# One block for the gated update and the three convolutions of a graph network

## The reference, cut to what matters

```
n   = relu(layernorm(x))
# layer 2: gated update
msg = segment_sum over edges of (n[src] @ W_msg.T + b_msg + edge_embed[edge_type])
r, z = sigmoid(...msg, n...);  new = tanh(i_n + r * h_n)      # GRU cell
x   = x + (1 - z) * new + z * n
n   = relu(layernorm(x))
# layer 3: three graph convolutions with symmetric norm (dinv = 1 / sqrt(degree))
y   = conv(conv(conv(n)))        # relu after the first two
x   = x + y
```

## Time and profile before

| | us |
|---|---|
| median of 3 runs | 6237.64 (6236.5 to 6240.86) |
| the profiled execution | 6241.27 |
| its span, first to last instruction | 6239.5 |
| PE busy | 4667.4 (75%) |
| POOL busy | 3137.0 (50%) |
| DVE busy | 2634.3 (42%) |
| ACT busy | 1472.9 (24%) |
| mean granted TensorE clock | 0.774 of full speed |

### The profile page before, as it was taken

How to read it: one execution, slowest core, us unless ns; L and a number is a source line. 1 busy time by engine, 2 the same in 40 slices (tenths; PEclk the granted TensorE clock), 3 DMA queues, 4 the chain that set the end, 5 groups by cost and what they waited for, 6 DMA issues and landing times. The chain is left out here.

```text
span 6239.5 us, 90775 instructions
## 1 busy us (share of the span) xinstructions
PE 4667.4 (75%) x25783; PEld 3126.0 (50%) x25784; DVE 2634.3 (42%) x6089; ACT 1472.9 (24%) x2786; POOL 3137.0 (50%) x3319
## 2 busy tenths in 40 slices
PE   5555555555555548888888888888899799999998
PEld 3444444444444435555555555555444444444444
DVE  6666666666666554444444444444312300000000
ACT  4211111111111123333333333333211211111000
POOL 3577777777777727777777777776000000000000
PEclk9555555555555568888888888888799899999999
DMA  6333333322333324444344434443345365555554
GB/s 218 110 94 94 94 94 94 92 87 84 93 94 94 105 80 125 132 133 133 125 131 133 133 123 133 133 133 96 136 159 162 99 200 191 187 193 190 192 193 150
DMA packets 337345, 817.56 MB, mean 131 GB/s; under 512 B 126590, under 2 KB 147633, under 8 KB 321059
## 3 DMA queue, kind: packets, MB, share of 16 engines
q1 hardware_dynamic: 217996, 516.64, 24.6%
q0 software_dynamic: 105568, 215.74, 12.7%
q10 hardware_dynamic: 13696, 84.07, 3.6%
HBM read 701.15 MB, written 114.23 MB: 131 GB/s over the span
## 5 line engine op out<-in xcount | busy, mean ns | idle before, releaser
L1388 POOL DMA_INDIRECT parts<-scratch_table,parts x1616 | 1541.2, 954 | 588.0 <-issue 480.1
L970 POOL DMA_INDIRECT parts<-scratch_table,parts x1616 | 1527.7, 945 | 554.5 <-issue 491.9
L185 PE MATMUL e_win<-parts 128*128 128x64 f32 x3232 | 783.0, 424 | 987.5 <-DMA parts<-scratch_table,parts 980.4
L185 PEld LDWEIGHTS e_win<-parts 128*128 128x128 f32 x3232 | 720.2, 328 | 1058.0 <-issue 1027.7
L1759 PE MATMUL c_sums<-ring,parts 128*128 128x512 bf16 (+1 forms) x3822 | 790.4, 368 | 21.0 <-ACT parts L2055 17.7
L1496 DVE TENSOR_TENSOR parts<-e_p,parts 128x512 f32<-128x512 f32 x404 | 279.4, 691 | 1160.5 <-PE e_p L1439 961.7
L185 PEld LDWEIGHTS e_win<-e_onehot,e_msg 128*128 128x128 f32 x3232 | 476.2, 211 | 245.3 <-issue 214.8
L1759 PEld LDWEIGHTS c_sums<-ring,parts 128*128 128x128 bf16 x3822 | 361.7, 98 | 430.1 <-issue 27.0
L1419 PE MATMUL e_p<-h,we 64*128 64x512 f32 x808 | 282.8, 772 | 365.7 <-DMA h<-in_edge_T 361.6
L222 DVE TENSOR_SCALAR parts<-e_iota,dst_rel,weight 128x64 f32<-128x64 f32 x1616 | 443.0, 335 | 254.8 <-issue 254.2
L1426 PE MATMUL e_p<-parts,we 128*128 128x512 f32 x808 | 518.0, 728 | 3.2 <-DVE parts L1503 2.9
(11 more groups left out here) (259 smaller groups left out, 4614.7 us busy)
## 6 DMA issues: line engine op xcount, KB each, us to landing
ring<-scratch_counts SPq DMA_DIRECT2D x336, 896.0 KB, 4.7
h<-in_time_rows SPq DMA_DIRECT2D x101, 1024.0 KB
parts<-scratch_table,parts POOLq DMA_INDIRECT x3232
h<-in_edge_T SPq DMA_DIRECT2D x101, 512.0 KB, 3.9
scratch_counts<-h ACTq DMA_DIRECT2D x12, 3136.0 KB
scratch_counts<-type_mem ACTq DMA_DIRECT2D x12, 3136.0 KB
scratch_table<-type_mem SPq DMA_DIRECT2D x33, 512.0 KB, 2.7
scratch_table<-parts SPq DMA_DIRECT2D x16, 512.0 KB
```

Of the source, the lines that this page charges most:

```text
L185: last = nc.tensor.matmul(win[:, 0:W], rows[:, j, :], onehot[:, j, :], start=(j == 0), stop=(j == J - 1))
L970: pool.indirect_dma_start(rows[:, half * NB + b, j, :], None, A["table0"], bass.IndirectOffsetOnAxis(ap=staged[:, half, b * J + j:b * J + ...
L1388: pool.indirect_dma_start(rows[:, half * NB + b, j, :], None, A["table1"], bass.IndirectOffsetOnAxis(ap=staged[:, half, b * J + j:b * J + ...
```

## The change

The two blocks become one, with one ring of counts, one set of PSUM banks (`pO` is `pM`) and one clearing of 91 semaphores at the end. Buffers are shared: `y`, `gap` and `bmsg` lie in `new_in` and `pre`, `emb` in `ones`, and the three `piece_gap` buffers in `digit_ring` and the second half of `square`. All 13 loads of weights are issued at the start, and the first bias addition waits for all of them. ScalarE copies the aggregate first in a step. The norm factors are made in three parts: tiles 0 to 39 at the start of step 11 (with the scaling of pieces 0 to 4), tiles 40 to 43 at step 12 (with piece 5), tiles 44 to 48 at the end (with piece 6). The splits of the first pieces stand between the two halves of step 12's ScalarE and VectorE work. TensorE makes the gates of chunk 12 inside the first convolution's chunk 0, ahead of piece 2.

```diff
-            ring = sbuf(st, "ring3", [P, PIECES, 2, PT, HALF], BF16)
...
+            y, gap, bmsg = new_in, pre, pre[0:TP, 0, :]
+            piece_gap = [digit_ring[:, k, :, :]... for k in range(2)] + [square[:, 1, :, :]]
+            pO = pM
+            tiles_of_norm = (slice(0, 40), slice(40, 44), slice(44, NT))
+            def last_but_one(c):
+                return isinstance(c, int) and c == whole_chunks - 1
...
             @block.sync
             def _(sp):
+                load_counts(sp, s3, loaded, ring, digit_ring)
                 for conv in range(CONVS):
-                    load_counts(sp, of_conv[conv], counts_loaded[conv], ring, digit_ring, of_conv[conv - 1] if conv else None)
+                    load_counts(sp, of_conv[conv], counts_loaded[conv], ring, digit_ring,
+                                *((of_conv[conv - 1],) if conv else (s3, (s_part[2], PIECES))))
...
             @block.tensor
+                def update(c, k, tiles, before):
+                    if tiles:
+                        product(pe, s3, above3, loaded, ring, digit_ring, parts[0], sums, c, k, tiles, False)
+                        if before:
+                            gates(c, k, before)
+                        else:
+                            pe.wait_ge(weights_in[0], all_weights)
+                            pe.wait_ge(s3["bias"], 2)
+                def last_gates():
+                    gates(whole_chunks + 1, 1, last_tiles)
+                run_chunks(update)(pe)
+                pe.wait_ge(s3["out"], whole_chunks + 2)
...
                                 product(pe, s, above, counts_loaded[conv], ring, digit_ring, parts[0], sums, c, k, tiles, True,
-                                        (s_part[2], [j + 1 for j in range(PIECES)]))
-                                pe.wait_ge(weights_in[0], w_base + 32 * CONVS)
+                                        (s_part[2], [j + 1 for j in range(PIECES)]), last_gates)
...
             @block.scalar
+                def root(i):
+                    act.wait_ge(s_norm, 4 * i + 1)
+                    nc.scalar.activation(std[:, tiles_of_norm[i]], var[:, tiles_of_norm[i]], ACT.Sqrt).then_inc(s_norm, 1)
+                def split(first, end):
+                    for j in range(first, end):
+                        if j < PIECES:
+                            act.wait_ge(s_h0, j + 1)
+                            nc.scalar.activation(left_parts[0][:, piece(j), :], h[:, piece(j), :], ACT.Copy).then_inc(s_part[0], 1)
+                        for k in (1, 2):
+                            if 0 <= j - k < PIECES:
+                                act.wait_ge(s_gap[k - 1], j - k + 1)
+                                nc.scalar.activation(left_parts[k][:, piece(j - k), :], piece_gap[(j - k) % 3],
+                                                     ACT.Copy).then_inc(s_part[k], 1)
+                def update(c, k, tiles, before):
+                    s = s3
+                    if last_but_one(c):
+                        root(0)
+                    if tiles:
+                        act.wait_ge(s["used"], c * PIECES + 2 * PIECES)
+                        nc.scalar.activation(agg[:, k, 0:tiles * P], sums[:, k, 0:tiles * P],
+                                             ACT.Copy).then_inc(s["out"], 1)
+                    if before:
+                        if tiles == last_tiles:
+                            root(1)
+                        ... mT, hT
+                        if tiles == last_tiles:
+                            split(0, 4)
+                        ... Sigmoid, Tanh, Square
+                        if tiles == last_tiles:
+                            split(4, 6)
+                run_chunks(update)(act)
+                root(2)
+                split(6, PIECES + 2)
...
             @block.vector
+                dve.wait_ge(weights_in[0], all_weights)
+                def scale(i, first, end):
+                    at = tiles_of_norm[i]
+                    dve.wait_ge(s3["ssq"], (at.stop + 3) // 4)
+                    ... var, reciprocal, times dinv of these tiles
+                    for j in range(first, end):
+                        nc.vector.scalar_tensor_tensor(h[:, piece(j), :], ...).then_inc(s_h0, 1)
+                def split(first, end):
+                    for j in range(first, end):
+                        if 0 <= j - 2:
+                            g = piece_gap[(j - 2) % 3]
+                            dve.wait_ge(s_part[1], j - 1)
+                            nc.vector.tensor_tensor(g, g, left_parts[1][:, piece(j - 2), :], ALU.subtract).then_inc(s_gap[1], 1)
+                        if 0 <= j - 1 < PIECES:
+                            dve.wait_ge(s_part[0], j)
+                            if j >= 4:
+                                dve.wait_ge(s_part[2], j - 3)
+                            nc.vector.tensor_tensor(piece_gap[(j - 1) % 3], h[:, piece(j - 1), :],
+                                                    left_parts[0][:, piece(j - 1), :], ALU.subtract).then_inc(s_gap[0], 1)
+                def update(c, k, tiles, before):
+                    if last_but_one(c):
+                        scale(0, 0, 5)
+                    if tiles == last_tiles:
+                        scale(1, 5, 6)
+                        split(0, 4)
+                    if before:
+                        gru(c - 1, before)
+                    if tiles:
+                        ... held
+                    if before:
+                        center(c - 1, before)
+                    if tiles == last_tiles:
+                        split(4, 6)
+                run_chunks(update)(dve)
+                scale(2, 6, 7)
+                split(6, PIECES + 2)
```

More of the change, by code:

```diff
@@ L1716, in counts_in, with load_counts @@
                     src.rearrange("h p (t d) -> (h p) t d", d=HALF)[:, :, 0:tiles * P])
-        def load_counts(sp, s, loaded, ring, digit_ring, last=None):
+        def load_counts(sp, s, loaded, ring, digit_ring, last=None, split=None):
             flag_reg = sp.alloc_register(f"flag_{s['used'].name}")
@@ L1733, in chunk @@
                         sp.wait_ge(last["d_used"], (whole_chunks + 1) * (PLANES - 1) * PIECES + 1)
+                        if split is not None:
+                            sp.wait_ge(*split)
                     with sp.Fori(1, PLANES) as plane:
@@ L2061, in step @@
                     def step(c, half, tiles, before):
-                        k = (half + conv) % 2
+                        k = (half + conv + 1) % 2
                         if before:
@@ new lines, in center @@
+                def center(u, before):
+                    at = bass.ds(u * 4, before)
+                    dve.wait_ge(s["x"], u + 1)
+                    nc.vector.tensor_reduce(mean[:, at], x[:, at, :], AXX, ALU.add).then_inc(s["summed"], 1)
+                    dve.wait_ge(s["summed"], u + 1)
+                    nc.vector.scalar_tensor_tensor(h[:, at, :], mean[:, at].unsqueeze(2).to_broadcast([P, before, D]),
+                                                   -1.0 / D, x[:, at, :], ALU.mult, ALU.add).then_inc(s["centered"], 1)
+                    dve.wait_ge(s["squared"], u + 1)
+                    nc.vector.tensor_reduce(ssq[:, at], square[:, 0, 0:before, :], AXX, ALU.add).then_inc(s["ssq"], 1)
@@ new lines, in gru, with add_bias @@
+                def gru(u, before):
+                    dve.wait_ge(s["gates"], u + 1)
+                    b = slice(0, before)
+                    def add_bias(to, bank, part, row):
+                        for i in range(0, before, 2):
+                            n = min(2, before - i)
+                            pair = bank[:, i // 2, 0:n * 2 * D].rearrange("p (i g) -> p i g", i=n)[:, :, part]
+                            last = nc.vector.tensor_tensor(
+                                to[:, i:i + n, :], pair,
+                                row.unsqueeze(1).to_broadcast([P, n, part.stop - part.start]), ALU.add)
+                        return last
+                    add_bias(rz, pR, slice(0, 2 * D), bih[:, G2]).then_inc(s["rz_in"], 1)
+                    add_bias(pre, pN, slice(D, 2 * D), bhh[:, G1])
+                    add_bias(new_in, pN, slice(0, D), bih[:, G1]).then_inc(s["biased"], 1)
+                    dve.wait_ge(s["biased"], u + 1)
+                    dve.wait_ge(s["rz"], u + 1)
+                    nc.vector.tensor_tensor(pre[:, b, :], rz[:, b, 0:D], pre[:, b, :], ALU.mult).then_inc(s["v"], 1)
+                    dve.wait_ge(s["v"], u * 4 + 1)
+                    nc.vector.tensor_tensor(pre[:, b, :], pre[:, b, :], new_in[:, b, :], ALU.add).then_inc(s["pre"], 1)
+                    dve.wait_ge(s["new"], u + 1)
+                    at = bass.ds(u * 4, before)
+                    nc.vector.tensor_tensor(pre[:, b, :], h[:, at, :], new[:, b, :], ALU.subtract).then_inc(s["v"], 1)
+                    nc.vector.tensor_tensor(x[:, at, :], x[:, at, :], new[:, b, :], ALU.add).then_inc(s["v"], 1)
```

(4 more changed lines are left out.)

282 lines of the change are left out of this document (90 added, 192 removed).

## The result

The changed kernel takes **6217.98 us** (median of 7 runs, 6214.63 to 6219.32) against 6237.64 us (7 runs) before: ratio 0.9967, 95% interval 0.9957 to 0.9978, so 13.7 to 26.8 us faster. Forecast were 6215 us and 22.5 us less. The profiled executions differ by 26.2 us of span (6239.5 and 6213.3 us).

The account below looks back on a forecast made before the run. TensorE was taken to set the time inside the convolutions, with pauses at the seam before them. Seam terms gave 22.1 to 23.7 us, 23 taken, less 0.5 for clears: 22.5 us, median 6215 us, range 6210 to 6225.

Parts of the forecast that it names:

- Gates of chunk 11: Late update: aggregate copied first removes a 2.25 us wait; gates start at 4931.9, second half ends 4941.8 to 4945.6.
- First splits: Behind chunk 11's gate copies: pieces 0 and 1 split early; piece 0 starts 4945.0 to 4948.9, both done 4956.6 to 4961.3.
- Update of chunk 11: Queued behind the splits on VectorE and ScalarE: Sigmoid at 4947.7 to 4949.0, sum of squares done 4956.8 to 4958.1.
- The new wait: Last gates stand behind piece 2's wait for its parts: start 4960.7 to 4962.0, sum of squares 4971.8 to 4973.1.
- Last factors and piece 4: End of seam: piece 4's parts meet TensorE, piece 4 starts 4978.6 to 4980.2, chunk 0 ends 4992.2 to 4993.8.
- Semaphores: At the end, after the stores: 29 moved clears cost at most 2.6 us or 4.4 us; 0.5 us taken.
- What I costed at nothing: Six more weight loads before the bias additions, count loads and alternating table loads, all taken as hidden at no cost.
- The 2.25 us go: Gates of chunk 11: ScalarE copies the aggregate before older activations, so TensorE's 2.25 us wait disappears.
- A, double table loads: Three exposed ScalarE table loads at twice 1.28 us add 3.8 us: 6219 us; chance 0.12.
- B, low clock through the seam: TensorE stays at half clock until piece 4: gain 9.6 us less 0.5, time 6229 us; chance 0.05.
- C, no overlap: Some wait holds piece 0 until the last gates are done: saves 5 to 8 us, 6231 us; chance 0.06.
- D, slower: Low clock stays into convolution chunks 0 and 1: 63.5 us lost less 22.5, 6279 us; chance 0.03.

Follow-up runs that it names:

- The new order: Changed kernel with last gates ahead of piece 2's wait and only piece 6 and piece 5's third part split after the last factors; 7243.18 us, 0.9961 of before.
- aggregate first: Kernel before with only ScalarE's aggregate copy moved to the head of its step; 6226.44 us, ratio 0.9987 to before.
- one block: Changed kernel without early factors, early splits and last gates inside the product; 6225.95 us, ratio 0.9986 to before.
- factors: One merged block plus norm factors and scaling in three parts, all splits still at the end; 7265.44 us, one run.
- splits: Changed kernel with the last gates in their own step, ahead of the first convolution; 7262.26 us, ratio 0.9986 to before.
- the last kernel: Changed kernel with reordered last gates and splits, 76 semaphores cleared during the third convolution; 7236.80 us (0.9951 of before), repeated 7186.59 us (0.9959).

## Why the prediction was right, step by step

**Gates of chunk 11.** Their start, 4931.9, was measured at 4931.7 (4927.96 + 3.75), the end of the copies at 4936.3 (4936.3 to 4937.6 forecast), the end of the second half at 4943.5 (4941.8 to 4945.6 forecast). With the root ahead of the copies the second half ran partly at the low clock, as my upper end had it. All eight profiles with this root have the same pause and the same slow half.

**First splits.** Piece 0 starts at 4945.4 (4945.0 to 4948.9). The set-up took 1.97 us, not 3.25, and piece 0 ran at full clock: 4.69, not 6.4 to 7.2 us. Pieces 0 and 1 are done at 4955.3, a microsecond better than my good end. It gained nothing, for TensorE then stood in the new wait anyway (5.07 us). So the low clock that I put on piece 0 was wrong by 1.7 to 2.5 us, and the new wait covered the miss.

**Update of chunk 11.** Sigmoid at 4947.6 (4947.7 to 4949.0), end of the sum of squares at 4956.5 (4956.8 to 4958.1).

**The new wait.** The last gates start at 4960.4 (4960.7 to 4962.0), their sum of squares is done at 4971.3 (4971.8 to 4973.1). The new order, which takes this pause away and moves splits as well, has a seam 6.86 us shorter.

**Last factors and piece 4.** Piece 4 at 4978.0 (4978.6 to 4980.2), behind 1.66 us of pause. The good end of that range doesn't follow from my own terms, which give 4978.4 for the parts and 4978.9 for the pieces; the slip is 0.3 us at most. The rows of the last root:
```profile
4967.20 1.28 ACT L1963 ACT_TABLE_LOAD   x1
...
4968.50 0.21 ACT L1963 ACTIVATE std<-var 128x5 f32<-128x5 f32 x1
```
Chunk 0 ends at 4991.8 (4992.2 to 4993.8). So the seam gave 24.2 us where the sum said 22.1 to 23.7, and 23 was taken. The end lies 0.4 us before the early bound, as most of these times lie a little before theirs.

**Semaphores: the term that I mis-sized.** 0.5 us was taken, 1.83 measured, and a clear costs 0.063 us. I had leaned on the boundary of the earlier trace rows, "which holds much else", and given 29 clears a fifth of its 2.6 us; at 0.063 us each they are 1.84 of it. My upper ends, 4.4 and 2.6 us, held. This miss of 1.3 us and the 1.2 us by which the seam gave more than 23 cancel by luck: 22.5 measured in the trace, 22.5 forecast. The medians differ by 19.7 and 19.5 us in the two comparisons, about 3 less than the stages of the trace say. The intervals (13.7 to 26.8 in the first) hold the difference; no run explains it.

**What I costed at nothing.** The first gates of the update start 65.1 us behind the first product, 64.8 to 66.1 in the three profiles of before, so the six further weight loads stayed hidden. The update as a whole is not longer than in before's further profiles.

**What the total hid.** The single prices were right only for the whole. "The 2.25 us go" is 9.7 us when made alone, since the clock, `held` and the slow first piece hang on that pause. In the whole change part of that was given back: `root(1)` ahead of the copies brings a 1.87 us pause and the low clock again, 2.3 us together. I had both ends of the clock in the sum and so did not have to know this. The decomposition, in the order tried: aggregate first 9.7, one block 3.1, factors -1.8, splits 2.05, last gates inside chunk 0 11.15; together 24.2 us. It is one order of several, and the parts are not independent. So the theory that the overlap alone gives the 24 us was wrong, and so was its rival: the late aggregate with the slow products behind it is 9.7 us, the last gates inside chunk 0 are 11.15, and neither is most of it.

**Rivals.** A, double table loads: the load at 4942.52 begins 0.02 us behind a copy that ends at 4942.50, and Sigmoid follows at 4943.82, so 1.28 us and 0.02 us, behind a busy engine. What the Trainium skill states on a drain at each switch ("ScalarE: Activation LUTs", section "What ACT_TABLE_LOAD costs") is not borne out here. B, low clock through the seam: at 2.4 GHz from 4965 on, though it did fall in the 5.07 us pause. C, no overlap: two pieces ran before the last gates. I had priced it too low: with everything but that overlap the seam is 13.1 us shorter (84.10 - 71.04) and the tail 1.8 us longer, 11.3 us (9.3 by the medians) and not 5 to 8, again since the late aggregate weighs 9.7 us and not 2.25. D, slower: convolutions -0.1 us.

## What to carry to other kernels

A pause on TensorE costs itself and the slower products behind it, so look for the small wait (an aggregate copied behind activations that nobody needs yet) before building an overlap, and keep splits behind the copies that gates wait for, as the new order does. The same for a root ahead of such copies is an estimate, 2.3 us from the eight profiles; no run moved it. An overlap pays when the work that everyone waits for moves with it: here factors and splits moved early gave 0.2 us together, and the last gates moved between them 11. Count the clears that land behind the last store, 0.063 us each, and clear earlier what is no longer used.

## What the runs showed of the hardware that was not expected

- A semaphore clear on GpSimd takes 0.061 to 0.063 us (91 more: +5.77 us; 76 fewer behind the store: -4.64 us).
- The granted clock can fall behind pauses of only 1.2 us in the float32 gates: one in eleven second halves takes 6.9 to 7.0 instead of 5.34 us, in 12 of 13 profiles, at the first gates in five of them and at other steps in seven. What picks the step stays open. Behind the pause of 1.87 us the half was slow in eight profiles of eight.
- The first 21 products after a pause took 4.69 to 4.71 us in the ten cases with a pause of 1.5 to 2.15 us, 6.0 to 6.4 us in the three with 2.14 to 2.31 us, and at the boundaries of convolutions (3.1 to 3.7 us) 6.1 to 6.4 us, but for one of 26 that took 4.69. One kernel shows both at the same place.
- Two profiles of one kernel can differ by 3 us from the clock alone, so their spans don't tell a small edit. The stages repeat better: the seams of three profiles of before lie within 0.4 us, those of two of the changed kernel within 0.01, but those of the last kernel 1.4 us apart.
